# An attention and mixture-of-experts layer: score sums in four 32-column blocks of TensorE, head outputs regrouped by DMA, work moved between the vector engines

## The reference

```
q, k, v = x @ Wq.T, x @ Wk.T, x @ Wv.T          # 8192 tokens, 16 heads of 8
# attention inside one token: "N, S, D = x.shape", einsum over (token n, head q, head k)
att = softmax(einsum('nqhd,nkhd->nhqk', q, k) / sqrt(8));  x = LN(x + (att v) @ Wo.T + bo)
q, k = xpos(x), xpos(ctx)                        # retention, causal, with decay per head
x = LN(x + ((q k^T) * D) @ ctx)
x = LN(x + sum of the 2 chosen of 8 experts: (silu(x w1) * (x w3)) @ w2)
```

## Time and profile before

| | us |
|---|---|
| median of 3 runs (1247.94 to 1253.89) | 1248.9 |
| the profiled execution | 1250.01 |
| its span, first to last instruction | 1248.2 |
| TensorE busy in the span | 1086.2 |
| VectorE busy | 923.6 |
| GpSimd busy | 820.8 |
| ScalarE busy | 640.3 |
| mean granted TensorE clock | 0.903 of full speed |

### The profile page before, as it was taken

The page is one execution under the profiler, slowest core; times in us unless marked ns, Lnnn a source line. Parts: engine busy times, 40 slices in busy tenths (PEclk is TensorE's granted clock), DMA queues, the critical chain, the costliest instruction groups (busy, mean ns, idle before and its releaser), DMA issues. The chain is left out here.

```text
span 1248.2 us, 29396 instructions
## 1 busy us (share of the span) xinstructions
PE 1086.2 (87%) x8662; PEld 865.1 (69%) x8663; DVE 923.6 (74%) x2179; ACT 640.3 (51%) x1421; POOL 820.8 (66%) x1028
## 2 busy tenths in 40 slices
PE   4656999999999999999999999844999999999900
PEld 2445777777777777777777777533888888888800
DVE  3587758778788788788788776444888888888755
ACT  0224445455454554554554556413666666666625
POOL 0455966798888888888888988552444444444444
PEclk9878889999999999999999997656999999999955
DMA  8210000101101001101011010012222222222157
GB/s 267 56 33 18 26 18 18 42 29 35 44 27 48 30 29 41 31 30 42 30 32 38 24 35 23 19 50 63 63 56 58 58 59 59 59 57 59 42 180 236
DMA packets 80001, 67.51 MB, mean 54 GB/s; under 512 B 9664, under 2 KB 69184, under 8 KB 79936
## 3 DMA queue, kind: packets, MB, share of 16 engines
q1 hardware_dynamic: 59536, 36.65, 10.7%
q0 software_dynamic: 8704, 17.97, 4.5%
q10 hardware_dynamic: 11696, 12.08, 3.0%
HBM read 42.39 MB, written 24.28 MB: 53 GB/s over the span
## 5 line engine op out<-in xcount | busy, mean ns | idle before, releaser
L1446 POOL TENSOR_TENSOR prod_ev<-e_sb,q_v 128x512 f32<-128x512 f32 x256 | 319.6, 1281 | 86.7 <-DVE o_raw L1052 50.6
L513 PE MATMUL SC<-prod_qk,tab 128*128 128x256 f32 x1024 | 237.7, 386 | 4.5 <-DVE prod_qk L1022 2.6
L513 PEld LDWEIGHTS SC<-prod_qk,tab 128*128 128x128 f32 x1024 | 192.2, 193 | 32.2 <-issue 3.8
L1510 POOL DMA_INDIRECT token_halves<-w_new,tok_i x144 | 139.8, 971 | 38.2 <-issue 32.2
L1022 DVE TENSOR_TENSOR prod_qk<-q_v,QKV 128x2048 f32<-128x2048 f32 x64 | 146.0, 2281 | 18.2 <-ACT q_v L777 17.9
L586 PEld LDWEIGHTS ST<-ctx_bd,sm 128*64 128x64 f32 x2048 | 136.0, 149 | 29.7 <-issue 29.6
L529 PE MATMUL YY<-o_g,wo_sb 128*128 128x256 f32 x512 | 152.0, 463 | 0.0
L1469 POOL DMA_INDIRECT routed_rows<-xe,pos x128 | 128.2, 1002 | 33.9 <-issue 24.3
L586 PE MATMUL ST<-ctx_bd,sm 128*64 128x16 f32 x2048 | 142.2, 217 | 3.5 <-issue 3.5
L1052 DVE TENSOR_REDUCE o_raw<-prod_ev 128x128 f32<-128x2048 f32 x64 | 144.8, 2263 | 0.2 <-issue 0.2
L529 PEld LDWEIGHTS YY<-o_g,wo_sb 128*128 128x128 f32 x512 | 118.4, 237 | 23.2 <-ACT o_g L793 0.6
(11 more groups left out here) (153 smaller groups left out, 1857.6 us busy)
## 6 DMA issues: line engine op xcount, KB each, us to landing
w_new<-routed_rows SPq DMA_DIRECT2D x72, 130.0 KB
prod_ev<-token_halves SPq DMA_DIRECT2D x16, 512.0 KB, 4.8
x_sb<-x SPq DMA_DIRECT2D x32, 128.0 KB, 2.2
x_res<-x SPq DMA_DIRECT2D x64, 64.0 KB, 2.3
ctx_sb<-ctx SPq DMA_DIRECT2D x32, 128.0 KB, 2.4
ctx_bd<-ctx SPq DMA_DIRECT2D x64, 64.0 KB, 2.2
out<-prod_qk ACTq DMA_DIRECT2D x16, 256.0 KB, 4.1
token_halves<-w_new,tok_i POOLq DMA_INDIRECT x144
```

What stands on the lines that cost most here:

```text
L513: mm = eng.matmul(SC[:, 256 * u:256 * u + 256], ident, prod_qk[:, u, n, :], start=(n == 0 and u == 0), stop=(n == HD - 1), skip_group_chec ...
L1446: ins = eng.tensor_tensor(prod_ev[:, u, i:i + 4, :, :], e_sb[:, it.slot(2), u, NH * i:NH * (i + 4)].rearrange("p (i j) -> p i j", j=NH).un ...
L1510: eng.indirect_dma_start(out=halves, out_offset=bass.IndirectOffsetOnAxis(ap=tok_i[:, s, u:u + 1], axis=0), in_=yw[:, s, u, :], in_offset= ...
```

## The change

**Scores and projection on 32-column blocks.** `project` no longer makes one 128x384 product for each half. It takes 32 tokens as weights at a time, and four matmuls with 96 columns write the four 32-partition quarters of PSUM, one quarter of the features each: 32 matmuls for a duo. A quarter then holds two dims of all heads for its tokens, in `n` blocks. `scores` sums with a 128x32 matrix (`pick`), which also adds over the four quarters: 8 matmuls of 256 columns for each half, and each score row is spread over the four quarters, 4 keys in each.

**Softmax.** The maximum of a row is now partly in other partitions. Two matmuls (`half_over`, `quarter_over`) swap halves and quarters, and VectorE takes the maximum twice more. The subtraction is one VectorE instruction on PSUM. There is no VectorE sum of the weighted values any more: `sums` on TensorE adds them by sixteen 32x144 matmuls for each half, the exponentials copied beside the products by ScalarE (`beside`) giving the denominator.

**Head outputs.** `spread_heads`, and `attention_out` on both engines, are gone. SP writes the divided outputs `o_n` to DRAM (`head_rows`) and reads them back as `o_t`, two transfers of 128 partitions x 8 x 16 numbers, in runs of 16 numbers (64 bytes). `residual` multiplies by Wo. The duo's tokens then stand in another order, which the tables for cos, sin, the causal mask and the ids, and the loads of `x_res`, follow.

**Moved.** The six keys and queries instructions go from GpSimd to VectorE. The sum 1 + exp and the difference of logits go into ScalarE's `second_weight`. PSUM tensors are shared out anew, with waits (`wait_last`) that keep engines apart which use one PSUM bank.

**Order.** All steps are ordered anew; the lags grow (TensorE 10 to 13), 20 steps are written out ahead of the loop, and `ctx_bd`, `x_res` and `o_t` wait for the duo just before, no longer for the one four back.

```diff
-    A_FIRST = 16
-    PE_LAGS, ACT_LAGS, DVE_LAGS, POOL_LAGS, SP_LAGS = 10, 9, 11, 13, 4
+    A_FIRST = 20
+    PE_LAGS, ACT_LAGS, DVE_LAGS, POOL_LAGS, SP_LAGS = 13, 11, 13, 10, 13
+    CTX_LAG, RES_LAG, HEADS_LAG, BD_LAG = 8, 9, 8, 13
...
+                if it := at(RES_LAG):
+                    r = it.slot(RING)
+                    wait(it, y_done, 1)
+                    for u in range(2):
+                        for b in range(2):
+                            eng.dma_start(x_res[S * u:S * u + S, r, b, :], x_rows[it.number()][u][b]).then_inc(x_res_in, 16)
+                    wait_dma(it, heads_out)
+                    wait(it, y_done, 1)
+                    for u in range(2):
+                        eng.dma_start(o_t[:, it.slot(2), u, :, :],
+                                      heads[r, u].rearrange("(g t) (d h) -> (t d) g h", t=NH, d=HD)).then_inc(heads_in, 16)
+                if it := at(HEADS_LAG):
+                    wait(it, on_ready)
+                    eng.dma_start(heads[it.slot(RING)].rearrange("u p c -> p u c"),
+                                  o_n[:, it.slot(2), :, :, :].rearrange("p u d h -> p u (d h)")).then_inc(heads_out, 16)
+                if it := at(BD_LAG):
+                    r = it.slot(RING)
-                    wait(it, o_done[1], RING)
+                    wait(it, o_done[1], 1)
                     for b in range(2):
-                        eng.dma_start(ctx_bd[S * b:S * b + S, r, :, b, :], ctx_rows[it.number()][b]).then_inc(ctx_in[r], 16)
+                        eng.dma_start(ctx_bd[S * b:S * b + S, r, :, b, :], ctx_rows[it.number()][b]).then_inc(bd_in, 16)
...
-                for n in range(HD):
-                    mm = eng.matmul(SC[:, 256 * u:256 * u + 256], ident, prod_qk[:, u, n, :],
-                                    start=(n == 0 and u == 0), stop=(n == HD - 1), skip_group_check=True)
+                for n in range(2):
+                    for g in range(4):
+                        mm = eng.matmul(SC[QUARTER * g:QUARTER * g + QUARTER, 256 * u:256 * u + 256].rearrange("p (q i j) -> p q i j", q=4, j=4),
+                                        pick, prod_qk[:, u, n:HD:2, :].rearrange("p q (i j) -> p q i j", j=NH)[:, :, :, 4 * g:4 * g + 4],
+                                        start=(n == 0 and u == 0), stop=(n == 1), skip_group_check=True)
...
+            def sums(it, u):
...
+                for j in range(4):
+                    for q in range(4):
+                        mm = eng.matmul(SUMS[QUARTER * q:QUARTER * q + QUARTER, u, :], pick,
+                                        prod_ev[:, u, q, j, :, :].rearrange("p i d -> p (i d)"), start=(j == 0), stop=(j == 3))
+                mm.then_inc(sums_done[u], 1)
...
             def ret_values(it, u):
                 wait(it, sm_ready[u])
                 if u == 0:
                     wait(it, sm_ready[1])
-                    wait_ring(it, ctx_in, per=48)
+                    wait_dma(it, bd_in, per=32)
```

More of the change, by code:

```diff
@@ L106, in count, with total @@
         return self.snaps[key]
+    def total(self, per, back=0):
+        n = self.off + 1 - back
+        if self.i is None:
+            return per * n
+        assert n > 0
+        key = (per, UNROLL, n)
+        if key not in self.snaps:
+            self.snaps[key] = self.eng.snap((self.i * UNROLL + n) * per)
+        return self.snaps[key]
     def ring_count(self, per, back=0):
@@ L124, in wait, with wait_dma, wait_last @@
     item.eng.wait_ge(sem, item.count(back))
+def wait_dma(item, sem, back=0, per=16):
+    if item.i is None and item.off + 1 - back <= 0:
+        return
+    item.eng.wait_ge(sem, item.total(per, back))
+def wait_last(item, n, *before):
+    if item.i is not None:
+        sem, back = before[0]
+        assert item.off - back < n - (n - item.off) % UNROLL
+        item.eng.wait_ge(sem, item.count(back))
+        return
+    for sem, back in before:
+        if 0 <= item.off - back < n:
+            item.eng.wait_ge(sem, item.off - back + 1)
+            return
 def wait_ahead(item, sem, ahead, n):
@@ L156, in run_steps, with build @@
         alone(s)
-def build(nc, x, ctx, w_qkv, wo_by_token, bo, gate, w1, w3, w2, table, where, out):
+def build(nc, x, ctx, w_qkv, wo, bo, gate, w1, w3, w2, table, where, out):
     n_tok = x.shape[0]
@@ L634, in step @@
+                if it := at(12):
+                    rows_across(it)
+                if it := at(3):
+                    scores(it, 1)
+                if it := at(11):
+                    ret_values(it, 1)
+                if it := at(13):
+                    ranks(it)
+                if it := at(10):
+                    before_ret_scores(it, 0)
                 if it := at(5):
-                    keys_across(it)
-                if it := at(9):
-                    gates(it)
+                    sums(it, 0)
@@ L1042, in one_over @@
[L1042 to L1052 removed]
+                wait(it, half_done, 1)
+                wait(it, two_ready, 1)
@@ L1065, in norm_shift, with queries @@
+            def queries(it):
+                wait(it, xqb_ready)
+                wait(it, qt_done, 1)
+                eng.tensor_tensor(xq[:, :, :], xq_a[:, :, :], xq_b[:, :, :], ALU.add).then_inc(xq_ready, 1)
             def norm_shift(c, d):
@@ L1434, in queries, with weighted @@
[L1434 to L1445 removed]
+            def weighted(it, u, half):
+                if half == 0:
+                    wait(it, e_ready)
+                    wait(it, sums_done[u], 1)
+                for q in range(2 * half, 2 * half + 2):
```

600 lines of the change are left out of this document (296 added, 304 removed).

## The result

| | median, us | range of the runs | ratio to before, 95% interval |
|---|---|---|---|
| before, beside it | 1251.4 | 1247.9 to 1254.7 | |
| after | 1629.9 | 1619.9 to 1630.6 | 1.3004, 1.2947 to 1.3060 |
| predicted | 1450 | 1300 to 1600 | |

Slower, as forecast, but 180 us more than the number and 30 us beyond the upper end. The profiled execution of after took 1619.9 us.

What follows compares the result with a forecast made beforehand. A chain through four queues was taken to bound each step: 1.2 + 12.0 + 3.7 + 8.9 = 25.8 us, plus 3.1 for the clock, 28.9. Then 1250 + 766 - 590 + 25 = 1451, forecast 1450 us, range 1300 to 1600.

Steps and rivals of the forecast that it cites:

- The chain: Four queues pass one dependency loop per duo, from ret_scores through head_rows and ctx_bd to the next ret_scores: 28.9 us.
- Item 1: From ret_scores on TensorE to the start of mask on VectorE: 1.16 us, summed as 1.2.
- Item 2: VectorE from mask to the end of divide: 10.2 us of work, 0.5 and two waits for TensorE, together 12.0.
- 3. SyncE to `ret_values`: SP issues head_rows and the ctx_bd load, which lands with its semaphore: 3.7 us, ends 2.9 and 5.0.
- item 4: TensorE from ret_values to the next ret_scores, with second_residual on VectorE between: 8.9 us, plus 3.1 for the clock.
- 0.4, the first maximum needs `sums` of the second half: VectorE's wait for TensorE ahead of its first maximum, between mask and divide: 0.4 us.
- the clock's price: Low TensorE clock after its idle hole adds 1.4 for ret_values, 0.9 for scores, 0.8 for the rest: 3.1 us.
- The packed blocks: Four 32-column matmuls on TensorE overlap fully: scores 1.8, sums 2.1 and projection 1.4 us per duo.
- The rival without overlap: TensorE's 32-column blocks do not overlap: 37.5 us a step, 1679 us; 8 in 100, half for partial overlap.
- The clock stays full: TensorE's clock never falls: 25.8 us a step, 1369 us; held within the likeliest case, 76 in 100.
- The open chain: ctx_bd lands ahead of ret_values, leaving a VectorE loop of 18 us a step: 1162 us; 13 in 100.
- The break-even of 21.3: Step length in us where 26.5 steps plus 25 equal 590; below it the kernel is faster than before.

Runs made afterwards that it cites:

- bd_ahead: Against after, the two ctx_bd loads alone moved ahead of x_res, o_t and head_rows in SyncE's queue: 1255.4 us on one chip, 1333.2 on the other.
- bd_between: Against after, the ctx_bd loads moved behind x_res and o_t but ahead of head_rows in SyncE's queue: 1351.7 us.
- w2_scatter: Against after, second_weight moved behind divide and GpSimd's indirect DMAs behind its second product run, SyncE's queue unchanged: 1472.4 us.
- single moves: Against after (1628.5 us), second_weight alone moved behind divide: 1550.2; GpSimd's indirect DMAs alone moved behind its second product run: 1559.6.
- group 1: Against after, on a chip later groups did not use: ctx_bd loads, second_weight, indirect DMAs each moved alone, then together: 1255.4, 1474.7, 1554.8, 1173.0 us.
- all three moves: Against after, ctx_bd loads ahead in SyncE's queue, second_weight behind divide, indirect DMAs behind GpSimd's second product run: 1173.0 us on one chip, 1178.0 on the other.
- bd_scatter: Against after, ctx_bd loads ahead in SyncE's queue and indirect DMAs behind GpSimd's second product run, second_weight unmoved: 1240.5 us.

## Why the prediction was wrong

**The chain: right.** All its links are in the trace, and `bd_ahead`, which touches one queue's order, takes 295 of the 379 us (1628.5 less 1249.3) away. That the link is `head_rows` and not the long list of loads is shown by `bd_between`: with the loads behind `x_res` and `o_t`, but ahead of `head_rows`, the time is 1352 us, and ahead of them all it is 1333 on the same chip.

The items, against a step of after (872.59 to 910.13) and one of `w2_scatter`, `mask` at 478.86 and at 509.67:

| | predicted | after | both holds gone |
|---|---|---|---|
| 1. `ret_scores` to `mask` | 1.2 | 1.8 | 2.1 |
| 2. `mask` to the end of `divide` | 12.0 | 19.7 | 12.4 |
| 3. SyncE to `ret_values` | 3.7 | 3.4 | 3.8 |
| 4. `ret_values` to the next `ret_scores` | 8.9 + 3.1 | 12.6 | 12.6 |
| the step | 28.9 | 37.5 | 30.8 |

The rows of `w2_scatter` for the last column, on VectorE and TensorE:

```profile
490.63 0.59 DVE L1140 TENSOR_TENSOR o_n<-YY,r_den 128x256 f32<-128x256 f32 x1
...
509.67 1.23 DVE L1197 TENSOR_TENSOR sm<-ST,tab 128x1024 f32<-128x1024 f32 x1 [2.33 <-PE ST L645]
```

```profile
495.02 3.60 PE L658 MATMUL ST<-ctx_bd,sm 128*64 128x16 f32 x32 [8.13 <-DMA ctx_bd<-ctx]
...
507.61 1.99 PE L645 MATMUL ST<-q,k_t 64*64 64x512 f32 x8
```

**Item 2: this is the step that failed.** It was predicted at 12.0 us and measured 19.7. Its work was priced right, 12.4 without the two holds. It left out both: the hold by GpSimd's products and the late signal, which cost 78 and 69 us by single moves and 156 together, of the 180 missed. The price of 0.34 us for each of the six instructions of 256 columns was the gap from the start of a `second_residual`, with one operand in PSUM, to the next start. All six have both in SBUF, and GpSimd's second product run begins beside them, because `second_weight`, which releases it, stands right ahead of them. In the step above three of them and the first one-hot each last until one of the four products has ended: 0.85 + 1.0 + 0.96 + 0.78 = 3.6 us over what they take alone. (With the 4.3 us ahead of `m_two` that is 0.6 more than the 7.3 between 19.7 and 12.4; the step of `w2_scatter` has small waits that are so much longer.) In other steps one of them is held by all four: `xk_a` took 5.17 us at 699.00, until the last of GpSimd's four products was over:

```profile
699.00 5.17 DVE L1148 TENSOR_TENSOR xk_a<-ctx_sb,tab 128x256 f32<-128x256 f32 x1
```

```profile
699.37 4.51 POOL L1525 TENSOR_TENSOR prod_ev<-e_sb,q_v 128x512 f32<-128x512 f32 x4
```

`mask`, 1.22 us at 872.59 with one operand in PSUM, lies beside GpSimd's other run, from 871.42, and is not held. The Trainium skill has this rule: "SBUF — State Buffer", section "Who interferes with whom", says that a VectorE instruction with two SBUF inputs contends with a GpSimd instruction that reads SBUF, and that with at most one, outside what it calls the 2-port modes, it doesn't. The trace agrees, 1.38 us for `xk` beside the products against 0.42, and `mask` unheld. The hold was there to be read in before as well, on the same one-hot: the first `oh` took 1.0 to 1.1 us in 14 of 23 duos, always until the end of a product, and 0.16 to 0.18 in the other 9, with no product beside it. One of the 14, two instructions in the row, with the products that end at 243.80:

```profile
242.75 1.18 DVE L1126 TENSOR_TENSOR oh<-tab,ix 128x16 f32<-128x16 f32 x2
```

```profile
238.87 4.93 POOL L1446 TENSOR_TENSOR prod_ev<-e_sb,q_v 128x512 f32<-128x512 f32 x4 [0.90 <-DVE o_raw L1052]
```

In before VectorE had slack, busy in 77 of 100 us. On the chain the hold counts: without it the steps go from some 37.6 to 34.2 us and the time falls by 78.

**The other part of item 2** is "0.4, the first maximum needs `sums` of the second half". The wait is there, but 4.3 us long in some 20 steps, and the move that ends it is worth 69 us. No row read from before showed such a wait.

**Item 1** went with the clock. `ret_scores` comes some 12.6 us behind the hole in TensorE and took 1.74 us in the step of after and 1.99 in that of `w2_scatter`, instead of 1.09. I put the clock's price into item 4 alone: 0.9 was missed there, and 0.6 in item 4; with 0.4 in item 2 that is the step of 30.8 for 28.9. By the sum it would be 50 us more than 1450, and 22 were measured: only some 24 steps have the full length, where 26.5 were counted, and the last seven fall from 28.6 to 16.5 us. So a part of the nearness of 1472 to 1450 is luck: steps too short, but too many of them.

**The packed blocks: right.** At the full clock `scores` took 1.07 us (0.9 predicted), `sums` 1.19 (1.04), the projection 1.53 (1.4), here in `bd_ahead` of group 1:

```profile
491.00 1.19 PE L594 MATMUL YY<-prod_ev,tab 128*32 128x144 f32 x32
...
493.15 1.53 PE L555 MATMUL QKV<-w_qkv_sb,x_t 128*32 128x96 f32 x64
...
496.58 1.07 PE L567 MATMUL SC<-prod_qk,tab 128*32 128x256 f32 x16
```

16 records of 256 columns took 3.70 us before. Two sums of the prediction beside the chain do not come out: 22.7 - 15.9 + 9.1 is 15.9 us of TensorE and not 17, and no overlap at all would add three times 1.8 + 2.1 + 1.4, which is 15.9 and not 12. Neither is in the 1450. The rival without overlap, 1679, came closest to the measured time, for a reason that has nothing to do with it: a time near a rival's is no evidence for the rival.

**The clock stays full: refuted,** 0.70 in the window and 3.60 us for the first `ret_values` of the step against 2.04 for the second.

**The open chain,** priced at 18 a step and 1162 us, is what `bd_ahead` makes. Its steps were 22.4 to 25.5 on the chip without the late signal, where the hold by GpSimd's products stayed; with all three moves they are mostly 17 to 21.5, and the time is 1173 and 1178. The break-even of 21.3 was too low, by the same count of steps: `bd_scatter`, mostly at 22.2 to 23.3, is 1% faster than before.

## What to carry to other kernels

Look for a wait that closes a loop over several queues before looking at work: here a load placed behind a write in one queue was worth 295 of the 379 us lost. Price an instruction on such a chain by a row with its own kind of operands (SBUF or PSUM) and name what runs beside it on GpSimd; slack hides in before what becomes full cost on the chain. When variants are compared with a kernel, measure that kernel again beside them on the same chip: two of my differences were off by about 80 us until I did.

## What the runs showed of the hardware

- What waited for TensorE's signal at the end of `sums` came 3.1 to 4.7 us late in 14 to 21 of 32 steps on one chip and in the result's trace, always with GpSimd's indirect DMAs begun 1.4 us or more ahead of it, and in none on another. Other signals of TensorE passed during the same DMAs: in the step of after where `m_two` started at 694.40, just behind the first of the four at 694.34, `m_sb` with TensorE's matmul between followed at 695.74. The kernel before has the same time on both, 1251.9 and 1251.5 us.
- A VectorE instruction of 128x256 with both operands in SBUF, 0.42 us alone, took 1.2 to 1.4 us when it ended behind one of GpSimd's products, and 4.8 to 5.4 when it ended behind the last of four that follow each other: GpSimd's next ones may pass it.
